# A decoder layer on one core: side jobs of cross attention moved to other steps, ScalarE writes the rounded parts, and experts and combine become one unrolled stage

## The reference

```python
x = _layernorm(x + self_attention(x))                      # 16 heads, decayed linear attention
x = _layernorm(x + cross_attention(x, ctx_1024))           # 16 heads of 16, 1024 keys, softmax
x = _layernorm(x + ffn(x))

def ffn(x):                                                # 32 experts, each picks its 8 best tokens
    logits = einsum('bsd,ed->bse', x, gate_w) + gate_b
    probs = softmax(logits, axis=-2)
    vals, idx = top_k(probs over tokens, 8)
    merged = einsum('bked,bke->bed', x[idx], vals)         # one row of 256 for each batch and expert
    h = gelu([merged, 1] @ w1[e])                          # w1: 32 x 257 x 1024
    o = [h, 1] @ w2[e]                                     # w2: 32 x 1025 x 256
    out = zeros.at[idx].add(o * vals)                      # weighted rows back to the picked tokens
```

## Time and profile before

| | us |
|---|---|
| median of 3 runs (1977.33 to 1981.59) | 1978.41 |
| the profiled execution's own time | 1978.7 |
| its span, first to last instruction | 1976.7 |
| TensorE busy | 1748.2 (88%) |
| VectorE busy | 1258.2 (64%) |
| ScalarE busy | 861.0 (44%) |
| GpSimd busy | 545.4 (28%) |
| mean granted TensorE clock, share of full | 0.924 |

### The profile page before, as it was taken

The page is one execution under the profiler, slowest core; times in us unless marked ns, Lnnn a source line. Parts: engine busy times, 40 slices in busy tenths (PEclk is TensorE's granted clock), DMA queues, the critical chain, the costliest instruction groups (busy, mean ns, idle before and its releaser), DMA issues. The chain is left out here.

```text
span 1976.7 us, 48744 instructions
## 1 busy us (share of the span) xinstructions
PE 1748.2 (88%) x19756; PEld 835.5 (42%) x19756; DVE 1258.2 (64%) x2425; ACT 861.0 (44%) x1036; POOL 545.4 (28%) x658
## 2 busy tenths in 40 slices
PE   6999999999985688989999999999999899976665
PEld 3666666666653133333423433433333333322324
DVE  6667767766743867778678668668677778810005
ACT  3334333433321155645456456446456455651213
POOL 3545564555435132140140140320320300000002
PEclk8999999999996599999999999999999999987675
DMA  6000000000001211202101111112012013246982
GB/s 234 3 3 4 3 3 3 3 3 3 3 3 46 78 41 49 70 8 68 47 26 49 47 50 37 35 50 66 6 50 70 1 61 124 87 171 249 422 360 99
DMA packets 60085, 135.21 MB, mean 68 GB/s; under 512 B 11120, under 2 KB 34192, under 8 KB 51696
## 3 DMA queue, kind: packets, MB, share of 16 engines
q1 hardware_dynamic: 55152, 127.90, 17.7%
q10 hardware_dynamic: 4736, 4.46, 0.7%
HBM read 89.20 MB, written 4.98 MB: 48 GB/s over the span
## 5 line engine op out<-in xcount | busy, mean ns | idle before, releaser
L1567 DVE TENSOR_REDUCE mx<-cpsV 128x1 f32<-128x512 f32 x1024 | 651.3, 684 | 232.8 <-PE cpsV L1270 217.4
L1471 ACT ACTIVATE w<-cpsA 128x1024 f32<-128x1024 f32 x512 | 496.3, 1021 | 378.7 <-PE cpsA L1338 378.6
L1270 PE MATMUL cpsV<-w 96*128 96x512 bf16 x1024 | 339.5, 403 | 65.8 <-DVE mx L1567 51.6
L1292 PE MATMUL cacc<-w 128*32 128x512 f32 x2048 | 282.4, 617 | 0.4 <-ACT w L1471 0.4
L1338 PE MATMUL cpsA<-w 99*128 99x512 bf16 x1024 | 278.2, 394 | 0.3
L1270 PEld LDWEIGHTS cpsV<-w 96*128 96x128 bf16 x1024 | 84.8, 99 | 380.7 <-DVE mx L1567 220.4
L1128 POOL TENSOR_TENSOR w<-w,zero 128x1024 bf16<-128x1024 f32 x21 | 39.7, 1892 | 647.0 <-ACTq L1444 647.0
L606 ACT COPY QK<-psA 128x1024 f32<-128x1024 f32 x64 | 64.8, 1013 | 228.4 <-PE psA L363 228.4
L1338 PEld LDWEIGHTS cpsA<-w 99*128 99x128 bf16 x1024 | 99.6, 100 | 130.2 <-issue 15.1
L714 POOL TENSOR_TENSOR VP<-V,VPF 128x128 f32<-128x128 f32 (+2 forms) x256 | 128.8, 534 | 41.4 <-PE psA L376 36.1
L363 PE MATMUL psA<-XT,wq 128*128 128x512 f32 x256 | 130.6, 634 | 4.7 <-issue 2.9
(11 more groups left out here) (214 smaller groups left out, 2361.8 us busy)
## 6 DMA issues: line engine op xcount, KB each, us to landing
w<-in_w SPq DMA_DIRECT2D x64, 1024.0 KB, 17.6
w<-w SPq DMA_DIRECT2D x192, 128.0 KB, 2.3
w<-w SPq DMA_DIRECT2D x192, 64.0 KB, 2.0
w<-in_ctxT SPq DMA_DIRECT2D x8, 1024.0 KB, 4.9
XT<-in_xT SPq DMA_DIRECT2D x8, 512.0 KB, 6.5
x_tok<-in_x SPq DMA_DIRECT2D x8, 512.0 KB, 10.2
out_y<-y ACTq DMA_DIRECT2D x8, 512.0 KB, 2.9
wq<-in_WqT SPq DMA_DIRECT2D x1, 1024.0 KB, 10.8
```

What stands on the lines that cost most here:

```text
L1270: nc.tensor.matmul(out, Qst[q // 2][0:ROWS, hh, g * P:(g + 1) * P], Kst[q // 2][0:ROWS, hh, half * BANK:(half + 1) * BANK], start=True, st ...
L1292: last = nc.tensor.matmul(acc[BLK * jj:BLK * (jj + 1), :], Vc[:, c, 4 * q + jj, :], Pr[:, (2 * s + jj // 2) % 4, (jj % 2) * T:(jj % 2 + 1) ...
L1471: nc.scalar.activation(Pr[:, (2 * s + pp) % 4, :], src, ACT.Exp, scale=CA_SCALE).then_inc(act_evac, 1)
L1567: nc.vector.tensor_reduce(mx[:, q % 2, row, k % 2:k % 2 + 1], full(m[k]), AX_X, ALU.max).then_inc(dve_evac, 1)
```

## The change

1. Step numbers: `MERGE` 3 to 4, second `PROJECT_K` 11 to 12, `GATE` 11 to 13, `GATE_EXP` 13 to 15, `TOP8` 14 to 16, `TOP8_T` 15 to 17, `PICK` 16 to 28, `PICK_T` 17 to 29, `PROJECT_V0` 17 to 20. The section behind the last batch gets 30 steps, of which only those with a job do anything.
2. On TensorE `values` stands before the side jobs that ScalarE evacuates, in place of behind them.
3. ScalarE reads a projected block twice from PSUM: to R and, rounded to bfloat16, to the first part. PSUM counts as evacuated after the second copy. GpSimd makes three operations in place of four, each in four pieces of 256 columns; the copy of x and the bias on x are split in four as well. For the queries ScalarE waits for all stacking DMAs of the batch.
4. Experts and combine become one stage with the groups unrolled. The results don't go through DRAM: a matmul with a 0/1 table picks the rows of each group into one PSUM bank (four batches side by side on 32 partitions each). The output is worked off in 16 units of half a batch; a unit's matmuls use one of four groups of 32 rows, and each unit of four has a bank of its own. For six units TensorE adds x by a matmul with the identity and VectorE only takes statistics. The last w2 load is in two halves. The stage's first loads are 14 (before 4), and TensorE waits for the table and the bias rows before its first group.

```diff
-OUTPUTS, X1T, PROJECT_V1, PROJECT_Q, MERGE, PROJECT_O, NORM = 1, 0, 1, 2, 3, 5, 7
-PROJECT_K, X2T, COPY_X2, GATE, GATE_EXP, TOP8, TOP8_T, PICK, PICK_T = (7, 11), 9, 10, 11, 13, 14, 15, 16, 17
-PROJECT_V0 = 17
+OUTPUTS, X1T, PROJECT_V1, PROJECT_Q, MERGE, PROJECT_O, NORM = 1, 0, 1, 2, 4, 5, 7
+PROJECT_K, X2T, COPY_X2, GATE, GATE_EXP, TOP8, TOP8_T, PICK, PICK_T = (7, 12), 9, 10, 13, 15, 16, 17, 28, 29
+PROJECT_V0 = 20
...
-            ops.tensor_tensor(high, r, zeros, ALU.add)
+            for c in range(pieces):
+                ops.tensor_tensor(cut(r, c), cut(r, c), cut(high, c), ALU.subtract)
             eng.drain()
-            ops.tensor_tensor(r, r, high, ALU.subtract)
+            for c in range(pieces):
+                ops.tensor_tensor(cut(mid, c), cut(r, c), zeros, ALU.add)
             eng.drain()
-            ops.tensor_tensor(mid, r, zeros, ALU.add)
-            eng.drain()
-            ops.tensor_tensor(low, r, mid, ALU.subtract)
+            for c in range(pieces):
+                ops.tensor_tensor(cut(low, c), cut(r, c), cut(mid, c), ALU.subtract)
             eng.drain().then_inc(parts_ready, 1)
...
+                    if now and s:
+                        pe.wait_ge(act_evac, CA_ACT.count(sec, b, ("s", s - 1, 1)) + 2)
+                        values(b, s - 1)
                     if now and s == PROJECT_V1:
                         project_v(1)
...
-                    if now and s:
-                        pe.wait_ge(act_evac, CA_ACT.count(sec, b, ("s", s - 1, 1)) + 2)
-                        values(b, s - 1)
...
-                    nc.scalar.copy(R[:], src).then_inc(act_evac, 1)
+                    if n == 2 and sec != "pro":
+                        for q in range(QUADS):
+                            act.wait_ge(stacked[q], b * STACKED + STACKED)
+                    nc.scalar.copy(R[:], src)
+                    if n < 2:
+                        nc.scalar.copy(KP[:, n, 0, :], src).then_inc(act_evac, 1)
+                    else:
+                        nc.scalar.copy(QP[:, :, 0, :], src.rearrange("p (h t) -> p h t", h=2)).then_inc(act_evac, 1)
                     act.drain().then_inc(whole_ready, 1)
...
+            def pick_rows(n):
+                pe.wait_ge(o_evac, n + 1)
+                for h in range(2):
+                    for j in range(BT):
+                        last = nc.tensor.matmul(psS[E * j:E * (j + 1), h * D:(h + 1) * D],
+                                                pick[:, BT * h + j, E - EG - EG * n:2 * E - EG - EG * n], og[n % 2][:],
+                                                start=(n == 0 and h == 0), stop=(n == GROUPS - 1 and h == 1),
+                                                skip_group_check=True)
+                last.then_inc(picked, 1)
...
+            def combine(s):
+                for g in range(2):
+                    for j in range(BT):
+                        u = BT * s + j
+                        b, half, bank = unit(u)
+                        t0, rows = (2 * half + g) * P, slice(E * j, E * (j + 1))
+                        last = nc.tensor.matmul(bank[:, g * D:(g + 1) * D], p8[rows, b // BT, t0:t0 + P], oall[rows, b // BT, :],
+                                                start=(u not in X_BY_PE), stop=True, skip_group_check=True)
+                last.then_inc(full, 1)
...
+            pe.wait_ge(c_loaded, 16 * (1 + BT))
             pe.wait_ge(zeroed, 1)
...
+                last.then_inc(h_full, 1)
+                if n:
+                    pick_rows(n - 1)
...
+                if n == GROUPS - 1:
+                    pe.wait_ge(b1_ready, 1)
+                    for u in (0, 1):
+                        add_x(u)
...
+                nc.scalar.copy(og[n % 2][:], psO[n % 2]).then_inc(o_evac, 1)
-                    act.drain().then_inc(o_evac, 1)
-                    for j in range(EG):
-                        act.dma_start(sh.o_dram[bass.ds(it * (2 * EG) + (EG * n + j), 1), :], og[n][BLK * j:BLK * j + B, :]
-                                      ).then_inc(o_saved, 16)
-                    act.wait_ge(o_saved, it * 128 + (n * 64 + 64 + 32))
```

More of the change, by code:

```diff
@@ L1006 @@
 LEAD = 12
-TAIL_STEPS = 18
+TAIL_STEPS = 30
 CA_SCALE = HD ** -0.5
@@ L1518, in add_bo @@
             def add_bo(b):
-                nc.gpsimd.tensor_tensor(xb(b), xb(b), bo[:].unsqueeze(1).broadcast_to([P, G, D]), ALU.add
-                                        ).then_inc(bo_added, 1)
+                for g in range(G):
+                    last = nc.gpsimd.tensor_tensor(xb(b)[:, g], xb(b)[:, g], bo[:], ALU.add)
+                last.then_inc(bo_added, 1)
             def body(sec, b):
@@ L1528, in body @@
                 if nxt:
-                    nc.gpsimd.tensor_tensor(xs[:], xb(b + 1), zero[:].unsqueeze(2).broadcast_to([P, G, D]), ALU.add
-                                            ).then_inc(xs_ready, 1)
+                    for g in range(G):
+                        last = nc.gpsimd.tensor_tensor(xs[:, g], xb(b + 1)[:, g], zero[:].broadcast_to([P, D]), ALU.add)
+                    last.then_inc(xs_ready, 1)
                     pool.drain()
@@ new lines, in _ @@
+            pick_rows(GROUPS - 1)
+            pe.wait_ge(p_loaded, 16 * B)
+            pe.wait_ge(z_ready, GROUPS)
+            pe.wait_ge(oall_ready, 1)
+            combine(0)
+            pe.wait_ge(oall_ready, 2)
+            combine(1)
+            for u in (10, 11, 8, 9):
+                if u - 8 in X_BY_PE:
+                    pe.wait_ge(y_ready, (u - 8) // 2 + 1)
+                else:
+                    pe.wait_ge(summed, added_before(u - 8))
+                add_x(u)
+            combine(2)
@@ new lines, in _ @@
+            for v in range(UNITS // 2):
+                act.wait_ge(rstd_ready, v + 1)
+                for u in (2 * v, 2 * v + 1):
+                    _, _, bank = unit(u)
+                    for g in range(2):
+                        src = bank[:, g * D:(g + 1) * D] if u in X_BY_PE else y[:, u, g, :]
+                        at = 2 * u + g
+                        last = nc.scalar.activation(y[:, u, g, :], src, ACT.Identity, bias=shift[:, at:at + 1],
+                                                    scale=rstd[:, at:at + 1])
+                last.then_inc(y_ready, 1)
@@ new lines, in _ @@
+            for u in range(UNITS):
+                b, half, bank = unit(u)
+                if u % BT == 0:
+                    dve.wait_ge(full, u // BT + 1)
+                src = bank.rearrange("p (g d) -> p g d", g=2)
+                if u not in X_BY_PE:
+                    nc.vector.tensor_tensor(y[:, u], src, sh.x[:, G * b + 2 * half:G * b + 2 * half + 2, :], ALU.add
+                                            ).then_inc(summed, 1)
+                    src = y[:, u]
+                dve.drain()
+                for g in range(2):
+                    nc.vector.bn_stats(stats[:, g, :], src[:, g, :])
+                dve.drain()
+                for g in range(2):
+                    last = nc.vector.bn_aggr(mv[:, u, g, :], stats[:, g, :])
+                if u % 2:
+                    last.then_inc(var, 1)
@@ L1925, in decoder_layer @@
             cross_attention(nc, sh, dram)
[L1926 to L1931 removed]
+            experts_and_combine(nc, sh, dram, out)
 def _heads_inner(w):
```

308 lines of the change are left out of this document (135 added, 173 removed).

## The result

The changed kernel takes 1914.07 us (median of four runs, 1913.65 to 1914.79) and the kernel before 1979.71 beside it: a ratio of 0.9669, with an interval of 0.9653 to 0.9686. That is faster, and 3 us from the forecast of 1911. The span went from 1976.7 to 1911.7 us, 65.0 less, and the mean granted clock from 0.924 to 0.952.

The account below looks back on a forecast made before the run. TensorE sets cross attention's pace, losing time to stops at VectorE's bursts and a lower clock; weight loads bound the experts. Cross attention -60 and experts with combine -7 take 1978.7 to 1911 us; own range 1897 to 1925, stated range 1889 to 1944.

Parts of the forecast that it names:

- the main term: Cross attention: side jobs cover TensorE's stops at VectorE's bursts and the clock stays at 2.4 GHz; gains 14.2 us a batch.
- the sum: Per batch of cross attention: -14.2 (6.1 of it clock), +0.7 gate, +1.05 order of `values`, +3.0 second copy, making -9.5 us.
- My signs of being wrong: Prediction wrong if clock rows show lower stretches in cross attention, or a batch's window is over 134 us.
- The first: Rival: clock keeps falling twice a batch, as new waits of 1.3 us replace the stops; 1946 us, chance 0.15.
- the fourth: Rival: slower than before, TensorE's waits after side jobs each drawing a stretch at 1.2 GHz; 2033 us, chance 0.03.
- The second: Rival: each of a burst's three operations waits for its own piece, step 4 stops 1.6 us; 1939 us, chance 0.12.
- the limit: Expected profile of a cross attention batch: no stop over 1.4 us before L1270's successor.
- the rule cited in the prediction: VectorE operations with two SBUF inputs block fully against a GpSimd operation reading SBUF, for the whole instruction.
- The third: Rival: the second copy costs nothing and TensorE's waits with it go; 21 us less, 1890 us, chance 0.11.
- The fifth: Rival: VectorE's stops have another cause than GpSimd, only covered bursts and the end gain; 1978 us, chance 0.03.
- the 0.5 us of stop that I allowed: Step 4: 0.5 us of stop left from 3.0, with the output's transposes as cover; gain 2.9 us.
- The term that failed by most: Experts' end: two add_x jobs between transposes and product with w2 take 1.85 us where 1.1 was idle; +1.3 us.

Follow-up runs that it names:

- the tenth: Changed kernel with both the old step numbers and `values` back behind the side jobs; second copy, pieces and new end stay: 1919.72 us, ratio 0.9688.
- the second: Changed kernel with GpSimd making the first part again in four pieces, and one ScalarE copy: 1894.95 us, ratio 0.9568.
- the third: Changed kernel with ScalarE freeing PSUM after the first copy and rounding the first part from R in SBUF: 1899.29 us, ratio 0.959.
- The fourth experiment: Changed kernel with TensorE's wait for the experts' small loads moved down to the first picking of rows: 1910.82 us, ratio 0.9646.
- the fifth run: Changed kernel with the old step numbers for the side jobs, all else as changed: 1924.49 us, ratio 0.9718.

## Why the prediction was right, and where its sizes were off

**The steps and the clock.** This was the main term, and it holds. Step 5 lost the 2.93 us that I had put down to the clock. Steps 13 and 14 are back at the full clock too, but hold the gate now, so their share can't be read off by itself. TensorE's work in the fourth batch fell by 6.2 us, and 6.1 was in the sum. The steps alone, without pieces, gave 50 us, where the whole change gave 65. That this comes from covering the stops is shown by the runs with one part each: counted in windows of 3 us up to the end of the last batch, cross attention had 13 stretches with a clock under 0.85 before, 17 with the pieces alone, five with the steps alone, three in the changed kernel with whole pieces, two in the tenth, one each in the second and the third, and none in the changed kernel. Behind the last batch the clock is low in both kernels, and a little lower in the changed one; I had left that part out. My signs of being wrong spoke of lower stretches in cross attention as a whole, and there they are met, but not in the batches that the term is about.

**The rivals.** The first and the fourth fell: the batch holds waits of 1.44, 1.23 and 1.17 us behind the copies, and the clock in it is 1.00. The second was half right as a mechanism: three operations of the burst did meet a piece each (0.52, 0.50 and 0.65 us). One of them is the CAST, which has one input. But step 4 lost 0.49 + 0.30 us by it and not 1.6, and no clock. Only the first batch, which has no transposes in step 4 to cover the burst, stops for 1.49 + 0.30 us, more than the 1.4 that I had set as the limit, and its clock stays full. For the two operations with two inputs (0.50 and 0.65 us) the rows agree with the rule cited in the prediction (the Trainium skill, SBUF — State Buffer, section Who interferes with whom); the third such operation lasted 0.16 us and met no piece, and the CAST is not covered by the rule as the prediction gives it. What the block cost was less, since a piece is 0.64 us long. The third fell: the copies cost what was said. The fifth fell with the batch at 131.97.

**Per batch: -7.9 measured, -9.5 predicted.** From one step 0 to the next, steps 0 to 10 went from 58.26 to 55.72 us (-2.5, where the sum's terms for these steps give -3.2), and the rest from 81.61 to 76.25 (-5.4, predicted -6.2). In the first half two sizes were off. The wait for the query's copies is 1.44 us, and step 2 got only 0.1 shorter, where the sum had 1.3 less 0.33. Step 4 takes 4.93 us, where my terms (5.84 - 2.5, with 0.96 for the transposes put into it) gave 4.3: the 0.5 us of stop that I allowed came to 0.79, and the rest isn't told apart. In the second half step 14 waits 0.89 us for VectorE behind the gate where I had 0.7; no run splits the rest. The waits for the copies themselves came as said, 3.8 us in three times where I had 1.3 each. The first section won 10.3 us in place of 6, of which 2.8 lie in the prologue, which I had at nothing. The sum by sections: five batches from the third on 39.8 (47 predicted), second 4.0 (5), first section 10.3 (6), last 1.0 (2), and the stretch behind it up to the experts 1.5 longer, which I had left out: 53.6 of 60. The total comes within 3 us of the forecast because the 4.5 us that the end won beyond its term make up for most of the 6.4 missing here; that part is luck.

**The costs.** Order of `values` and second copy stood in the sum at 1.05 and 3.0 us a batch, 28 in seven batches. Undone together, with the late wait for the small loads (3.3 by the medians), they give 29.0, that is 26 for the two: the sum was near. But they aren't separate terms: undoing either one alone gives 18 to 19 (15 where ScalarE keeps the second operation and reads R). The product with the values (1.1 us) is about as long as the second copy, and it can stand in only one of the two places; where it stands behind the job, it hides the copy's extra 1.0 us. I had priced the order for a kernel with one copy and the second copy with the order given; that sums right, and misleads whoever wants to undo one of them.

**The end: -11.5 measured, -7 predicted.** The wait for the small loads was 3.58 us (3.6 predicted), but the weight stream moved by less: the last group's first matmul comes 126.3 us behind the first small load in place of 123.9, 2.4 later where the sum had all of the 3.6. (The fourth experiment gave back the same 2.4 us of span.) The last group took 6.07 (5.64 predicted). The copy of hS stood right behind it, as said. The term that failed by most is the way from the transposes to the product with w2: 2.82 us against 4.4 in the sum, since the add_x job (1.89) runs beside the bias and the activation that this product waits for, and not ahead of them. Not foreseen: that product ran at the full clock, 3.66 us in place of 5.38, 1.7 won. From there to the first combine matmul 2.28 (2.4 predicted), to VectorE's first statistics 1.28 (2.0 predicted), and VectorE's chain 24.6 (24.5 predicted). The group of 32 matmuls in four row groups took 2.01 us for its 32 records. The add_x job's 8 records of the same 256 columns took 1.89 at the same full clock, so 32 one behind the other would take 7.6 by estimate, and the overlap is 3.8 times. The Trainium skill, TensorE: Matmul & The Clock Gate, section Measured speedup vs the span model, gives 3.07 for four row tiles: the overlap is confirmed, and larger here. The kernel with the end alone gives 9 by the medians and 13 by the profiled run's span, on either side of the 11.5, so the end adds to the rest as far as its scatter can tell.

**What is open.** The parts don't add: the steps alone give 50, the pieces alone 7 and the end alone 9, 66 in all, yet taking the steps away from the changed kernel costs 10 and the pieces 9. In the changed kernel the second copy covers a burst (seen for step 12 in the fifth run), so the steps are worth less there; a run with the old steps, all pieces and no second copy was not made.

Why a given stop is followed by the lower clock, no run settles, and its length alone doesn't decide it. With whole pieces, and again in the tenth run, the same stops to within 0.02 us were followed by a lower clock in some batches and by the full clock in others. The kernel before shows it too: in its second batch TensorE stood 2.32 and 0.30 us in step 4, as in the fourth, and step 5 behind it took 6.45 us at a clock of 1.00, where the fourth took 9.39. So the prediction's step from a stop to a fall of the clock holds for most batches of that kernel, not for each stop.

## What to carry to other kernels

When TensorE is bound and its clock is full but for a few stretches, look for the stop ahead of each stretch and put a job that is due anyway into it: here moving jobs by one to twelve steps gave 50 us. Shortening the rival engine's operations gave 7 to 9, and in one case moved an operation of GpSimd that was left whole onto another of VectorE, which cost as much as the pieces had won in a batch; cut all of them, and look at what each meets afterwards. When a step gets a longer evacuation of PSUM, first let the buffer go (read the second result from SBUF) and keep work between the job and the buffer's next use: that was 26 us that the changed kernel left lying (29 with the late wait for the small loads). Undo costs together as well as one at a time, since two that hide each other are each worth most of the sum.

## What the runs showed of the hardware that was not expected

- A CAST of 16 columns with one SBUF input lasted 0.52 and 0.48 us under GpSimd's pieces, and 0.17 and 0.19 in the kernel before; a TENSOR_SCALAR of 512 columns 2.42 us under a whole bias add, and 0.48 without. TENSOR_REDUCE from SBUF stayed at 0.19 us in the same bursts.
- Single waits of TensorE of 1.44, 1.23 and 1.17 us in one batch left its clock at 1.00, while 1.22 and 0.30 us close together were followed by 0.80 over 8.7 us in another kernel. Stops of 1.38 and 0.29 us in one batch were followed by a clock of 0.79 over the next step, and 1.37 and 0.29 in the next batch of the same run by 1.00.
- ScalarE's two reads of one PSUM buffer took 1.01 and 1.02 us, and started 0.91 us apart.
